# Mixture-of-experts stages of a perceiver kernel: first row tile selected by a matmul, next row tiles turned within the down projection, first weight pieces split ahead of the routing plan

## The reference

```python
# L0: top 1, at most int(512/8*1.25)+1 = 81 rows an expert; the rest are dropped
logits = xn @ wg;  e = argmax(logits);  gate = softmax(logits)[e]
y[t] = gate[t] * (gelu(xn[t] @ W1[e] + b1[e]) @ W2[e] + b2[e])

# L1: top 2, no limit; gates are a softmax of the two
logits = xn @ router_w.T + router_b
for e in range(8):
    h = silu(xn @ gate_w[e].T) * (xn @ up_w[e].T)
    out += (h @ down_w[e].T) * w[:, e]          # w is 0 where e was not chosen

x = x + that                                    # xn = layernorm(x)
```

## Time and profile before

| what | value |
|---|---|
| median of 3 runs | 3893.53 us (3889.25 to 3896.72) |
| profiled execution | 3890.58 us, its span 3889.3 us |
| L0 expert stage | about 1825 to 2084 us of the span |
| L1 expert stage | about 3288 us to the end |
| PE busy over the span | 3610.6 us (93%) |
| DVE, ACT, POOL busy | 65%, 49%, 46% |
| weight pieces loaded | 244, 1 MB each |

### The profile page before, as it was taken

The page is one execution under the profiler, slowest core; times in us unless marked ns, Lnnn a source line. Parts: engine busy times, 40 slices in busy tenths (PEclk is TensorE's granted clock), DMA queues, the critical chain, the costliest instruction groups (busy, mean ns, idle before and its releaser), DMA issues. The chain is left out here.

```text
span 3889.3 us, 46028 instructions
## 1 busy us (share of the span) xinstructions
PE 3610.6 (93%) x17868; PEld 2320.1 (60%) x17868; DVE 2531.3 (65%) x3462; ACT 1920.3 (49%) x1962; POOL 1775.6 (46%) x744
## 2 busy tenths in 40 slices
PE   7999999989999999986797999999999886799997
PEld 6777778755555555432674545555554475688886
DVE  3222234357777777637796877777776465699997
ACT  2112311245555555542683455555556321577775
POOL 1112111159999999920000599999998320100000
PEclk9999999999999999996897899999999998899999
DMA  7555565543333333102686233333331101799996
GB/s 274 181 180 178 189 197 173 176 133 91 86 87 77 85 87 87 38 23 109 272 358 211 55 83 91 85 87 79 85 87 30 49 1 44 289 372 369 377 379 251
DMA packets 215944, 593.83 MB, mean 153 GB/s; under 512 B 42624, under 2 KB 108192, under 8 KB 161840
## 3 DMA queue, kind: packets, MB, share of 16 engines
q1 hardware_dynamic: 176944, 517.47, 40.9%
q10 hardware_dynamic: 36864, 67.13, 4.6%
q0 software_dynamic: 1920, 6.29, 0.5%
HBM read 470.64 MB, written 120.09 MB: 152 GB/s over the span
## 5 line engine op out<-in xcount | busy, mean ns | idle before, releaser
L642 DVE TENSOR_REDUCE maxima<-psum 128x1 f32<-128x512 f32 x2048 | 1290.8, 683 | 387.3 <-PE psum L637 383.7
L751 ACT ACTIVATE pt<-psum 128x1024 f32<-128x1024 f32 x1024 | 1018.7, 1025 | 703.1 <-PE psum L662 697.6
L765 POOL TENSOR_TENSOR exp_sums<-pt 128x1024 f32<-128x1024 f32 x342 | 818.5, 2394 | 266.4 <-PE psum L678 132.4
L637 PE MATMUL psum<-ks,first_q 96*128 96x512 f32 x2048 | 815.0, 447 | 22.0 <-DMA first_q<-q_parts 9.2
L768 POOL TENSOR_TENSOR exp_sums<-exp_sums,pt 128x1024 f32<-128x1024 f32 x310 | 737.0, 2377 | 45.7 <-ACT pt L751 1.4
L637 PEld LDWEIGHTS psum<-ks,first_q 96*128 96x128 f32 x2048 | 394.3, 193 | 480.9 <-DVE maxima L642 326.0
L674 PE MATMUL psum<-pt,vs 128*32 128x512 f32 x4096 | 675.8, 600 | 4.7 <-DVE head_rows L778 2.3
L678 PE MATMUL psum<-exp_sums,constants 128*32 128x512 f32 x1408 | 671.7, 600 | 0.0
L662 PE MATMUL psum<-qs,ks 97*128 97x512 f32 x2048 | 648.7, 400 | 15.1 <-ACT pt L751 15.1
L1428 DVE TENSOR_TENSOR moe_cut<-moe_raw,moe_cut 128x2048 fp32r<-128x2048 f32 x244 | 557.1, 2291 | 55.6 <-ACT moe_cut L1370 50.9
L1370 ACT CAST moe_cut<-moe_raw 128x2048 fp32r<-128x2048 f32 x244 | 467.1, 1921 | 64.7 <-PE psum L97 64.7
(11 more groups left out here) (310 smaller groups left out, 4401.3 us busy)
## 6 DMA issues: line engine op xcount, KB each, us to landing
moe_raw<-in_moe_w SPq DMA_DIRECT2D x244, 1024.0 KB, 7.8
ks<-k_parts SPq DMA_DIRECT2D x384, 256.0 KB, 4.7
k_parts<-kparts ACTq DMA_DIRECT2D x256, 256.0 KB, 3.0
cx<-in_ctx SPq DMA_DIRECT2D x32, 1024.0 KB
v_heads<-vrow SPq DMA_DIRECT2D x32, 1024.0 KB, 5.8
vs<-v_heads SPq DMA_DIRECT2D x32, 1024.0 KB, 5.3
first_q<-q_parts SPq DMA_DIRECT2D x96, 64.0 KB, 4.1
qs<-q_parts SPq DMA_DIRECT2D x96, 64.0 KB, 4.8
```

The lines of the kernel that those rows point to most:

```text
L637: pe.matmul(self.c.bank[self.FIRST_BANK + k % 3], self.first_q[s][:, t * P:(t + 1) * P], self.ks[s][part][0:3 * DH, at:at + CHUNK], start= ...
L642: dve.tensor_reduce(self.maxima[:, h % 2, i % TT, i // TT:i // TT + 1], self.c.bank[self.FIRST_BANK + k % 3], X, ALU.max).then_inc(*self.f ...
L751: act.activation(self.pt[:, self.slot(h, b) + i:self.slot(h, b) + i + 2, :], self.c.psum[:, at:at + 2, :], ACT.Exp).then_inc(*self.exp.up())
L765: engine.tensor_tensor(to, self.pt[:, slot:slot + R, :], self.pt[:, slot + R:slot + 2 * R, :], ALU.add).then_inc(*signal.up())
```

## The change

Three things are done, in both expert stages.

1. The first tile's rows no longer come back from `x_slots`. `select_first_on_dve` multiplies expert 0's rank of each row with whether the row chose it, and compares iota + 1 with that, which makes a 0/1 matrix `select` of 128 rows by 128 slots for each of the four row blocks. `select_x` on PE multiplies the normalized rows with it: 16 matmuls of 128 by 128 by 128 in full f32, straight into the bank where `turn_x(0)` put its result. All rows, those of tile 0 too, still go to the slots. SP's wait for `x_sent` moves from tile 0 to tile 1, and the load of tile 0's rows goes.
2. `turn_x(j + 1)`, `x_high(j + 1)` and `x_low(j + 1)` move from ahead of the down projection to behind its second piece.
3. ACT's splits of pieces 0 to 2 move to right behind the copies of the normalized columns, ahead of the plan's exponential; DVE's splits of pieces 0 and 1 (`EARLY_LOWS` = 2) move to right behind the normalized rows, ahead of the router's best. DVE's split of piece 2 stays behind the plan.

```diff
+    EARLY_LOWS = 2
...
     def plan_top1_on_act(self, act):
         self.norm.on_act(act)
+        for g in range(self.AHEAD):
+            self.high_part(act, g)
         act.wait_ge(*self.plan.at(TT))
...
+    def select_first_on_dve(self, dve, chosen):
+
+        dve.tensor_tensor(self.first_rank[:], self.router.rank[:, :, 0], chosen, ALU.mult).then_inc(*self.first_ranked.up())
+        dve.wait_ge(*self.first_ranked.at(1))
+        for t in range(TT):
+            dve.tensor_scalar(self.select[:, t, :], self.c.iota[:], 1.0, self.first_rank[:, t:t + 1], ALU.add, ALU.is_equal).then_inc(*self.selected.up())
...
         self.norm.on_dve(dve)
+        for g in range(self.EARLY_LOWS):
+            self.low_part(dve, g)
...
         router.ranks_on_dve(dve)
+        self.select_first_on_dve(dve, hot[:, :, 0])
...
         router.ranks_on_dve(dve)
+        self.select_first_on_dve(dve, self.chosen[:, :, 0])
...
                 if w == (5 if j == 0 else 0):
-                    if j == 0:
+                    if j == 1:
                         sp.wait_ge(*self.x_sent.at(TT * self.choices))
                     if j > 1:
                         sp.wait_ge(*self.x_turned.at(j - 1))
-                    sp.dma_start(self.xrow[:, j % 2, :], xs[j * P:(j + 1) * P, :]).then_inc(*self.xrow_in[j % 2].up())
+                    if j:
+                        sp.dma_start(self.xrow[:, j % 2, :], xs[j * P:(j + 1) * P, :]).then_inc(*self.xrow_in[j % 2].up())
...
+        def select_x():
+            pe.wait_ge(*self.selected.at(TT))
+            for k in range(KD):
+                for t in range(TT):
+                    last = pe.matmul(bank[self.X_BANK][:, k * P:(k + 1) * P], self.norm.rows[:, t, k * P:(k + 1) * P], self.select[:, t, :], start=t == 0, stop=t == TT - 1)
+            last.then_inc(*self.x_turned.up())
...
-            if j + 1 < self.tiles:
-                turn_x(j + 1)
             if j:
                 pe.wait_ge(*self.y_done.at(j))
             for db in range(FB):
...
                 if db == 0:
                     turn_hidden(j, FB - 1)
-
-        turn_x(0)
+                if db == 1 and j + 1 < self.tiles:
+                    turn_x(j + 1)
+
+        select_x()
...
-            if j + 1 < self.tiles:
-                x_high(j + 1)
             for db in range(FB):
                 high(g + self.pieces - FB + db)
                 if db == 0:
                     leave_turned(j, FB - 1)
+                if db == 1 and j + 1 < self.tiles:
+                    x_high(j + 1)
...
-        for g in range(self.AHEAD):
+        for g in range(self.EARLY_LOWS, self.AHEAD):
             low(g)
         x_low(0)
...
-            if j + 1 < self.tiles:
-                x_low(j + 1)
             for db in range(FB):
                 low(g + self.pieces - FB + db)
                 if db == 0:
                     leave_turned(j, FB - 1)
+                if db == 1 and j + 1 < self.tiles:
+                    x_low(j + 1)
```

More of the change, by code:

```diff
@@ L1088, in run @@
             self.row_of = c.sb(st, f"row_of{l}", [P, self.choices, TT], U32)
+            self.first_rank = c.sb(st, f"first_rank{l}", [P, TT])
+            self.select = c.sb(st, f"select{l}", [P, TT, P])
             self.norm = Normalize(c, st, self.x, f"ln_m{l}")
@@ L1300, in on_pe @@
         c, bank, ht, cut, JB = self.c, self.c.bank, self.ht, self.cut, self.JB
+        def select_x():
[4 more added lines that the diff above has]
+            last.then_inc(*self.x_turned.up())
         def turn_x(j):
-            pe.wait_ge(*self.xrow_in[j % 2].at(j // 2 + 1))
-            if j:
-                pe.wait_ge(*self.xg_low.at(j))
+            pe.wait_ge(*self.xrow_in[j % 2].at((j + 1) // 2))
+            pe.wait_ge(*self.xg_low.at(j))
             for k in range(KD):
@@ L1355, in tile, with high_part, low_part @@
                     turn_hidden(j, FB - 1)
-        turn_x(0)
+                if db == 1 and j + 1 < self.tiles:
+                    turn_x(j + 1)
+        select_x()
         for j in range(self.tiles):
             tile(j)
+    def high_part(self, act, g):
+        act.wait_ge(*self.raw_in[g % self.RAW].at(g // self.RAW + 1))
+        if g >= self.CUT:
+            act.wait_ge(*self.used.at(g - self.CUT + 1))
+        act.copy(self.cut[:, g % self.CUT, 0], self.raw[:, g % self.RAW]).then_inc(*self.high.up())
+    def low_part(self, dve, g):
+        dve.wait_ge(*self.high.at(g + 1))
+        dve.tensor_tensor(self.cut[:, g % self.CUT, 1], self.raw[:, g % self.RAW], self.cut[:, g % self.CUT, 0].bitcast(F32), ALU.subtract).then_inc(*self.low.up())
     def on_act(self, act):
@@ L1364, in high @@
         def high(g):
[L1365 to L1370, removed]
+            if g < last_piece:
+                self.high_part(act, g)
         def x_high(j):
@@ L1397, in on_act @@
             act.wait_ge(*self.bias1_in.at(1))
-        for g in range(self.AHEAD):
-            high(g)
         x_high(0)
```

2 lines of the change are left out of this document (1 added, 1 removed).

## The result

| | before | after |
|---|---|---|
| median of four runs | 3892.99 us (3889.25 to 3896.72) | 3848.29 us (3841.60 to 3850.26) |
| ratio | | 0.9885, 95% interval 0.9873 to 0.9898 |
| profiled execution, its span | 3890.58, 3889.3 us | 3841.60, 3840.3 us |
| granted clock, mean of the span | 0.957 | 0.965 |

The account below looks back on a forecast made before the run. PE bounds both expert stages, so only its standing time can be gained: 10.0 + 14.8 + 1.2 + 8.0 = 34.0 us off, forecast 3858 us, range 3850 to 3872 (80%).

Parts of the forecast that it names:

- Term 3: First hidden matmuls of L0 and L1: PE may start at the upper clock level, gaining 1.2 us (0 to 4.1).
- Term 4: Later tiles of L0: turn behind the second down piece removes PE's six waits for `moe_xrow`, gaining 8.0 us (0 to 8.4).
- Term 1: First tile of L0: first hidden matmul at 1860.45 in place of 1870.45, gaining 10.0 us (7.9 to 12.0).
- Term 2: First tile of L1: first hidden matmul at 3324.7 in place of 3339.55, gaining 14.8 us (12.8 at the slower product price).
- faster by more: Whole kernel: chance 0.88 of a gain above 7.8 us, from the forecast, the turn, the starved tile and half of POOL's.
- POOL was not starved: Rival: POOL's scatters slowed by DVE's splits bring tile 1's rows late, 3884 to 3894 us, no gain left; 8%.
- No wait moved to `x_low`: Rival: in L0 ACT or DVE come late to `x_low`, or another engine binds; turn gains nothing, 3866 us; 10%.
- tile 0 did not starve: Rival: tile 0 starts early, then waits for splits of pieces 3 and later, losing the start and clock gains, 3882; 6%.
- the slower case: Rival: `x_low(j + 1)` behind one more DVE split makes PE stand 2.7 us before each of 21 tiles, 3922 us; 4%.

Follow-up runs that it names:

- the filling of the kernel before: Kernel before with unread matmuls filling PE's wait before tile 0, 16 in L0 and 24 in L1 (first try 14 and 22: 3889.84 us): 3886.87 us, ratio 0.9988.
- the second measurement: The kernel after measured once more with no edit: 3849.61 us, ratio 0.9894 against the kernel before.

## Why the prediction fell short: the places were right, the clock and the turn were priced too low

The forecast was 34.0 us; the stages gave 41.7. The steps that failed are two. Term 3 chose 1.2 us for the clock, near its lower end, where 3.9 were gained. Term 4 held that removing 8.4 us of waits can give 8.4 at most, where 10.4 were gained. Term by term:

| | forecast | measured | from |
|---|---|---|---|
| 1, first tile of L0 | 10.0 | 11.6 | openings |
| 2, first tile of L1 | 14.8 | 15.9 | openings |
| 3, clock | 1.2 | 1.3 + 2.6 | first tile of L0, 29.80 to 28.49; body of L1, 528.19 to 525.64 |
| 4, turn | 8.0 | 10.4 | the seven other tiles of L0, 176.40 to 166.02 |

A tile is taken here from store to store, the first one from the first hidden matmul.

**Term 1** was right in its steps. From the rank copy on I had 8.8 us, and it is 8.15, because the product took 5.53 us and not 6.2. The remaining 1.0 us lies ahead of it. The scores ran mostly at the full clock and took 4.22 us where they took 6.97, so they end at 1833.54; DVE's two splits end only at 1835.50, and the logits wait for them. They come 15.9 us after the stage's start instead of 16.9. With scores of 6.97 us they would have waited for PE until 1836.29, 0.8 us after the splits, which is the 0.8 to spare that I had. The size holds for this pair alone: with scores as fast as in the kernel with the turn alone, the opening before was 41.95 us, and the gain would be 8.6.

**Term 2** was right in its steps: the logits are 2.24 us late (forecast 3.05; the pieces landed 0.4 us sooner than in the earlier trace rows). DVE's split ends at 3274.81 and the scores, at the low clock this time, at 3274.66, so both hold them there. Then the way from the ranks to the first hidden matmul is 8.7 us (8.95). The two paths meet as I had it: PE's product ends at 3291.31 and DVE is free of its split at 3292.25.

**Term 3 is the largest error, 2.7 us of the 7.7.** I had the two ends right, 0 and 4.1, and took the value near the lower one, by the row with an idle of 2.2 us ahead of slow products. That step failed. What speaks for the upper end was in my own sum: a product of 6 us, full, and only 1.4 us of standing behind it. In L0 a stand of 1.46 us behind that product kept the clock in all seven kernels that had it, and 2.02 us (one early split) and 4.75 us (select alone) did not. In L1 stands of up to 2.21 us kept it, and those of 3.1 us and more lost it. It is no rule of the length alone: behind the filling of the kernel before, two stands of 1.4 us lost it in L0, and 1.52 and 1.40 us kept it in L1, as shown above. So the choice of 1.2 was a guess, and what decides between the ends stays open. My price of the slow stretch by its first matmuls, 1.4 and 2.7 us, was about right too. L0's first tile takes 28.4 to 28.5 us in the seven kernels that start fast. It takes 29.8 before, 30.1 with one early split and 31.0 with the turn alone, and the longer the stretch at 0.50 lasts, the more it takes. L1's bodies take 525.3 to 525.7 us where the clock holds and nothing is waited for, and 526.7 to 529.1 where it falls. In L1 the filled kernel shows that this is the clock; in L0 it is read from these pairs, since no run there removed the slow start alone.

**Term 4 was short by 2.4 us, and 2.0 beyond its own upper end.** The step that failed is "8.4 us waited, so 8.4 at most to be gained". In the kernel before, the wait that the weight loads show is longer (first fence), and the clock falls behind the 3.0 us wait (second fence, stretches of L0):

```profile
PEld psum L1307 <- DMA moe_xrow<-x_slots: 9.8, 6, 3.2
```

```profile
1911.40:1913.00 1.60, 1.45 (x6) 1.35 (x7) 0.78 (x2) 0.29 (x1) 0.00 (x0) 0.50 1.02 424
1913.00:1916.00 3.00, 3.00 (x12) 2.43 (x11) 1.56 (x2) 2.09 (x2) 0.00 (x0) 0.77 1.00 415
```

By these windows the clock costs up to 1.6 x 0.50 + 3.0 x 0.23 = 1.5 us, three quarters of the 2.0 us by which 10.4 exceeds 8.4. The last 0.5 us stays open. The run with the turn put back agrees: 9.2 us of waits and two such falls cost 13.1 us.

**The range.** Its low end summed the best ends, and two of these were too near: 8.4 for the turn, and 14.8 for L1, where I had allowed nothing better than the forecast. The stages alone would put the median at 3893.0 - 41.7 = 3851.3, within the range. The rest is 3.0 us (2.7 by the second measurement, where the gain was 43.9 and the stages gave 41.2). I have no cause for it. One possibility is code that the change doesn't touch: the start of L0's stage lies between 1818.7 and 1829.9 us over the fourteen profiled executions, with the same code up to there. Another is that the openings of the executions behind the medians differ from the profiled ones, by up to 3 us as shown above. Nothing here decides. The chances that I gave for "faster by more" also add up to 0.90, not 0.88.

**The rivals.** POOL was not starved. The first four scatters of L1 in the kernel after:

```profile
3289.80 1.03 POOL L1310 DMA_INDIRECT x_slots<-ln_m_rows,row_of  x1 [61.32 <-DVE row_of L1260]
3291.13 1.97 POOL L1310 DMA_INDIRECT x_slots<-ln_m_rows,row_of  x1 [0.30 <-issue]
3293.41 0.96 POOL L1310 DMA_INDIRECT x_slots<-ln_m_rows,row_of  x1 [0.30 <-issue]
3294.67 2.23 POOL L1310 DMA_INDIRECT x_slots<-ln_m_rows,row_of  x1 [0.30 <-issue]
```

The eight take 0.96 to 2.61 us, below the 3.3 at which the rival decides, and end at 3304.8. Those that start within a split end 0.83 to 0.85 us after it: the second at 3293.10, with DVE's split done at 3292.25. The 6.38 us scatter of before ended at 3325.06, 0.86 us after the last of three splits in a row, at 3324.20. But L0 of before has three splits in a row as well, and there each of the first three scatters stood only until the split then running was done. Behind the 2.32 us one come:

```profile
1858.31 1.74 POOL L1287 DMA_INDIRECT x_slots<-ln_m_rows,row_of  x1 [0.30 <-issue]
1860.36 1.88 POOL L1287 DMA_INDIRECT x_slots<-ln_m_rows,row_of  x1 [0.30 <-issue]
```

So a scatter waits for the split that it meets, and at some places to the end of the whole row. What makes the difference no run here shows. In tile 0 of the kernel after none stood for more than one split, and the rows of tile 1 were in time. The rule of the Trainium skill that I named (SBUF — State Buffer, Who interferes with whom) agrees with these rows in that the scatter that comes later stands until a split is done. The same section infers that a `tensor_tensor` does not stall the making of descriptors; the scatters here, which read their rows' numbers from SBUF, did stand.

The other three did not occur. No wait moved to `x_low` in L0 or L1, tile 0 did not starve (no wait of PE in it), and the slower case would have needed 1.2 us a tile where L1's steady run is 101.0 of 101 us busy. What term 4 missed was the clock behind the waits, not a new wait.

## What to carry to other kernels

Price a wait with what it does to the engine's clock behind it: in L0's tiles waits of about 1 us cost 1.1 to 1.4, and those of 2.3 to 3.0 us cost 3.7 to 4.0. When a transfer is taken off the path, look at once for the engine that comes last in its place (here DVE with its splits), since part of its work has to move ahead for the first edit to pay. And try the amount of what is moved ahead on both sides: one split too few made PE wait and cost 3.0 us of the stages, one too many made the plan late and cost 5.1. Last, compare a single profile's openings with care, since openings whose code was not touched moved by up to 3 us.

## What was not expected of the hardware

The 32 small matmuls of the scores (8 columns each) take from 3.89 to 6.97 us in the same code, by the granted clock. In the kernel before, L1, PE was busy for 2.88 of 3.00 us, and fell to the low level all the same, where it was busy for 2.19 of 2.30 us:

```profile
3298.00:3301.00 3.00, 2.88 (x23) 2.91 (x23) 0.00 (x0) 1.27 (x1) 0.00 (x0) 0.87 1.02 429
3301.00:3303.30 2.30, 2.19 (x11) 2.10 (x10) 0.00 (x1) 0.00 (x0) 0.00 (x0) 0.50 1.02 431
```

Matmuls put ahead of them did not settle it: with the same filling, L0's scores took 4.98 us in one kernel and 6.97 in another. What sets their level is open. In the profiled executions of before and after they went 6.97 to 4.22 us in L0 and 5.07 to 6.97 in L1. So some of the openings' difference is this and not the change: in L0 it is the 1.0 us of the 11.6 by which the logits came sooner.
